# A four-part graph network: the maximum chain two groups ahead, f16 counts, two of twelve scatters behind attention

## The reference

```
h = relu(layernorm(x)); x = x + L0(h)      # graph attention
h = relu(layernorm(x)); x = x + L1(h)      # 5 rounds of sums over edges, product, batch norm
h = relu(layernorm(x)); x = x + L2(h)      # sum over edges by source, mean
h = relu(layernorm(x)); x = x + L3(h)      # message network and a gated unit
# L0, with two head groups (4 heads of 64, 8 heads of 32):
e  = leaky_relu(alpha_s[src] + alpha_d[dst], 0.2)
m  = segment_max(e, dst);  ex = exp(e - m[dst])
a  = ex / segment_sum(ex, dst)
out = segment_sum(h[src] * a, dst)         # then elu, times Wu, plus bias and residual
```

## Time and profile before

| what | value |
|---|---|
| median of 3 runs | 4940.51 us (4921.88 to 4944.49) |
| profiled execution | 4972.68 us, span 4971.0 us |
| TensorE / weight loads | 3609.4 us / 2384.7 us busy |
| VectorE / ScalarE / GpSimd | 2440.7 / 1053.0 / 2126.2 us busy |
| mean granted clock | 0.819 |
| POOL scatters in attention | 384, 647.5 us |
| POOL gathers in attention | 512, 549.6 us |

### The profile page before, as it was taken

One profiled execution on the slowest core, in us unless ns is written; L12 is line 12 of the kernel. 1 busy time (PEld: TensorE's weight loads), 2 busy tenths in 40 slices (PEclk: granted clock), 3 DMA queues, 4 the chain that ended last, 5 costly groups with the idle time before them and its releaser, 6 DMA issues. The chain is left out here.

```text
span 4971.0 us, 63954 instructions
## 1 busy us (share of the span) xinstructions
PE 3609.4 (73%) x15754; PEld 2384.7 (48%) x15755; DVE 2440.7 (49%) x7725; ACT 1053.0 (21%) x2529; POOL 2126.2 (43%) x1886
## 2 busy tenths in 40 slices
PE   5566878777778754511127999999969788888889
PEld 3344555555555543300003555455545555665655
DVE  7766777777777765300001212222155456666656
ACT  0111222222222211200000202122034322222222
POOL 1366878877777850377661000000000055555520
PEclk9967777777777777655558999999979899999999
DMA  9277566556555665311122242322303233333330
GB/s 388 64 181 176 133 135 135 135 132 138 135 130 135 136 119 115 87 52 46 51 67 89 87 122 85 108 85 90 117 17 119 66 93 89 91 90 88 93 68 20
DMA packets 493099, 535.24 MB, mean 108 GB/s; under 512 B 225646, under 2 KB 396236, under 8 KB 492121
## 3 DMA queue, kind: packets, MB, share of 16 engines
q0 software_dynamic: 142000, 250.83, 21.7%
q1 hardware_dynamic: 338300, 266.64, 18.7%
q10 hardware_dynamic: 12749, 17.18, 1.4%
HBM read 470.80 MB, written 104.62 MB: 116 GB/s over the span
## 5 line engine op out<-in xcount | busy, mean ns | idle before, releaser
L1035 PE MATMUL p_out<-rows,hot 128*128 128x266 f32 x2048 | 820.3, 554 | 32.0 <-DVE rows L1157 24.1
L960 POOL DMA_INDIRECT count_dram<-number,place x384 | 647.5, 1686 | 203.7 <-issue 124.1
L1462 PE MATMUL p_lo<-cbuf,parts 128*128 128x400 f16 x1750 | 587.5, 336 | 92.4 <-issue 92.4
L1035 PEld LDWEIGHTS p_out<-rows,hot 128*128 128x128 f32 x2048 | 518.4, 273 | 227.4 <-DVE rows L1157 102.9
L1463 PE MATMUL p_hi<-cbuf,parts 128*128 128x400 f16 x1750 | 587.1, 336 | 47.7 <-issue 47.7
L952 POOL DMA_INDIRECT rows<-att_dram,idx x512 | 549.6, 1074 | 163.3 <-issue 146.8
L2031 POOL DMA_INDIRECT col_rows<-col_dram,m_idx x440 | 417.2, 948 | 435.2 <-ACT m_idx L2101 267.6
L1934 POOL MEMSET attr_w<- 128x512 f32 x1 | 0.5, 525 | 1271.7 <-POOLq L361 1271.7
L1531 POOL DMA_INDIRECT rec_dram<-records,edge_place x416 | 399.1, 959 | 166.6 <-issue 162.0
L1491 DVE TENSOR_TENSOR node_sum<-p_hi,low_sb 128x400 f32<-128x400 f32 x80 | 45.9, 574 | 806.9 <-ACT low_sb L1482 756.9
L1558 PE MATMUL l_p_turn<-wbot,hT 128*128 128x256 f32 x500 | 157.0, 450 | 270.1 <-issue 262.8
(11 more groups left out here) (383 smaller groups left out, 6445.3 us busy)
## 6 DMA issues: line engine op xcount, KB each, us to landing
cbuf<-by_src SPq DMA_DIRECT2D x40, 2500.0 KB
count_dram<-zeros SPq DMA_DIRECT2D x40, 1000.0 KB
dl_rep<-dl_dram SPq DMA_DIRECT2D x128, 256.0 KB
by_src<-count_dram POOLq DMA_DIRECT2D x25, 800.0 KB
g_rows<-by_src SPq DMA_DIRECT2D x25, 800.0 KB, 4.3
key_rep<-key_dram SPq DMA_DIRECT2D x64, 256.0 KB
rec_dram<-blank ACTq DMA_DIRECT2D x1, 14520.0 KB
m_attrs<-rec_dram SPq DMA_DIRECT2D x110, 128.0 KB
```

The costliest lines, as they stand in the source:

```text
L960: nc.gpsimd.indirect_dma_start(count_dram, bass.IndirectOffsetOnAxis(ap=place[r][:, n, c:c + 1].bitcast(U32), axis=0), number[r][:, 2 * n ...
L1035: m = nc.tensor.matmul(p_out[q][:, side, 0:HALF], hot[k][:, u, :], rows[k][:, u, side * HALF:(side + 1) * HALF], start=(u == 0), stop=(u = ...
L1462: nc.tensor.matmul(p_lo[m][:], parts[:, k, m, 1, :], cbuf[q][:, k, :], start=(k == 0), stop=(k == NT - 1))
```

## The change

Three things at once.

1. **Maximum chain.** Group j's pass runs the chain of j+2. TensorE's order in a pass is now: look-up of j+1, turn and turn back of j+2, first product of the sums, tops of j+2, the other products. `scale` has four buffers. The breaks `pen` have a semaphore of their own and are loaded two groups ahead, behind a wait for the scan of g. ScalarE makes the edge matrix of j+2 ahead of the exponential of j. Two groups' chains stand before the loop.
2. **Counts in f16.** `count_dram`, `zeros`, `number` are f16; `zeros` is 4000 wide, so 20 transfers fill the matrix. `by_src` is a view of `count_dram` and the copy goes. `LATE` is -256: a positive number marks the first of its key.
3. **Two of twelve scatters** of each turn (the second pair of k = 2) are kept in `place_post` and `number_post`. 27 of these 32 pairs go out in unify, 5 in the short block, each waiting for the one before. The order in the loop is now 4, 2, 2, 2.

```diff
+FIRSTS = (0, 4, 6, 8)
+IN_LOOP = 10
+POST = 2 * (GROUPS // 4)
+POST_UNIFY = 27
-LATE = 1024.0
+LATE = -256.0
-ZF = 2000
+ZF = 4000
-        zeros = sb("zeros", [P, ZF], F32, early)
+        zeros = sb("zeros", [P, ZF], F16, early)
-        count_dram = dram("count_dram", [KD + TRASH, 1], F32)
-        by_src = dram("by_src", [NP, NP], F16)
+        count_dram = dram("count_dram", [KD + TRASH, 1], F16)
+        by_src = count_dram[0:KD, :].rearrange("(p n) o -> p (n o)", p=NP)
+        def scatter_late(pool, first, last):
+            for n in range(first, last):
+                pool.wait_ge(placed, (CH - POST + 2 * n) * 16)
+                pool.nop().then_inc(waits_passed, 1)
+                for c in range(2):
+                    nc.gpsimd.indirect_dma_start(
+                        count_dram, bass.IndirectOffsetOnAxis(ap=place_post[:, n, c:c + 1].bitcast(U32), axis=0),
+                        number_post[:, n, c:c + 1], None, compute_op=ALU.add).then_inc(placed, 16)
 ...
 (SP)
+                        def breaks(g, q):
+                            for u in range(U):
+                                sp.dma_start(pen[q][u * HW:(u + 1) * HW, :],
+                                             pen_dram[...].partition_broadcast(HW)).then_inc(pen_in[q], 16)
                         def work(g, k, i):
+                            if within(g, 2):
+                                sp.wait_ge(run_ready, g + 1)
+                                sp.nop().then_inc(waits_passed, 1)
+                                breaks(g + 2, q)
                             if not (isinstance(g, int) and g < 2):
                                 sp.wait_ge(keys_used, g - 1)
-                            (four loads of pen)
 ...
 (ScalarE)
                         def work(j, k, i):
+                            if within(j, 2):
+                                edge_hot(j + 2, (k + 2) % 4)
                             act.wait_ge(arg_ready, j + 1)
                             nc.scalar.activation(slots(k), zz[:], ACT.Exp).then_inc(weight_ready, 1)
                             if within(j, 2):
                                 take_scores(j + 2, *after(k, i, 2))
-                                edge_hot(j + 2, (k + 2) % 4)
 ...
 (POOL: "if k % 2 == 0" becomes "if k == 0" for the two pairs of a step)
-                        pool.wait_ge(placed, CH * 16)
+                        pool.wait_ge(placed, (CH - POST) * 16)
 ...
 (TensorE)
                             if within(j, 1):
-                                turn(j + 1)
-                                turn_back(j + 1)
-                                node_tops(j + 1, (k + 1) % 4)
+                                look_up(j + 1, tiles[k])
+                            if within(j, 2):
+                                turn(j + 2)
+                                turn_back(j + 2)
                             if not (isinstance(j, int) and j < 2):
                                 pe.wait_ge(added, j - 1)
-                            for u in range(U - 1):
+                            add_up(j, k, 0)
+                            if within(j, 2):
+                                node_tops(j + 2, (k + 2) % 4)
+                            for u in range(1, U):
                                 add_up(j, k, u)
-                            if within(j, 1):
-                                look_up(j + 1, tiles[k])
-                            add_up(j, k, U - 1)
 ...
 (VectorE, the pass of group j, new order)
+                            if one:
+                                node_hot(j + 1, 1 - q, i1 * 2 + k1 // 2)      # now waits for dl_rep and keys
 ...
                             TS(zz[:], zz[:], 0.0, None, ALU.min).then_inc(arg_ready, 1)
+                            if one:
+                                alike(j + 1, k1, i1, 0)
+                                alike(j + 1, k1, i1, 1)
+                            if two:
+                                run_up(j + 2, q, i2 * 2 + k2 // 2)
+                            dve.wait_ge(weight_ready, j + 1)
+                            weigh(j, k, 0)
+                            n = scale_sums(j - 1, (k + 3) % 4, tile_before) if before else o.skip(1)
+                            if two:
+                                run_ends(j + 2)
+                            weigh(j, k, 1)
 ...
+                                add_sums(j - 1, 1 - q, tile_before)
+                            n = o.did(no_edge(j + 2)) if two else o.skip(1)
+                            weigh(j, k, 2)
+                            n = o.did(node_max()) if two else o.skip(1)
+                            if four:
+                                alike(j + 1, k1, i1, 2)
+                            n = o.did(group_max()) if two else o.skip(1)
+                            weigh(j, k, 3)
+                            n = o.did(with_own(tile_ahead)) if two else o.skip(1)
+                            o.did(edge_places(k, i))
+                            n = o.did(bent()) if two else o.skip(1)
+                            if four:
+                                alike(j + 1, k1, i1, 3)
+                            n = o.did(top_of(tile_ahead)) if two else o.skip(1)
+                            first = o.did(if_first(j + 1, k1, i1))
+                            falls(j + 2, q, tile_ahead)
+                            at_place(k1, i1)       # k1 == 2: second pair to number_post, place_post (two more small instructions)
+                            new_top(j + 2, tile_ahead)
 ...
 (unify, POOL)
-                        for t in range(NT):
-                            pool.dma_start(by_src[t * P:(t + 1) * P, :], counts[t * P:(t + 1) * P, :]).then_inc(narrowed, 16)
-                        pool.wait_ge(narrowed, 16 * NT)
+                        scatter_late(pool, 0, POST_UNIFY)
 (short block, POOL)
+                    scatter_late(pool, POST_UNIFY, POST // 2)
+                    pool.wait_ge(placed, CH * 16)
```

160 lines of the change are left out of this document (76 added, 84 removed).

## The result

The changed kernel took 5104.3 us (median of 4 runs, 5082.7 to 5114.4), the one before 4942.0 on the same chip: ratio 1.034, 95% interval 1.030 to 1.037. It is 3.4% slower; the prediction was 4850, faster. The profiled execution spans 5111.5 us against 4971.0.

What follows compares the result with a forecast made beforehand. The prediction took POOL, taken 96% of the time in attention, as the bound. Its terms, -84 - 3 + 4 + 1 - 5 = -87 us, brought the median from 4940.5 to 4853, stated as 4850, range 4805 to 4895.

Steps and rivals of the forecast that it cites:

- POOL sets the pace; the chain has some 10 us of slack.: Attention loop before the change: POOL, taken 96% of the time, bounds it; VectorE's places are ready some 10 us early.
- The chain, -84 us: Attention, 118 groups: maximum chain two ahead and two scatters out bring a group from 11.86 to 11.15 us, -84 us.
- from there to places and sums 6.7 us, near the full-clock end: New attention loop: from the scan to places and sums takes 6.1 to 8.0 us, taken as 6.7.
- VectorE alone is 10.0: Attention loop: VectorE's own work comes to 10.0 us a group, below POOL's.
- POOL's instructions unchanged: Attention loop: f16 scatters taken as long as f32 ones; denser VectorE work adds about 0.01 us to each POOL instruction.
- Keys on SP: 0: SP's new loading step in attention: lanes and keys there 9.4 us into the group, wanted at 11.3, so 0 us.
- Ahead of the loop, +4: Start of attention and its tail: a second chain ahead of the first places, one less at the tail, +4 us.
- Late scatters: Scatters moved behind attention: covered in unify, ending some 25 us early; five pairs in the short block cost +1 us.
- Zeros, -5: First block: f16 halves the bytes of zeros, so SP ends sooner and VectorE is last, -5 us.
- TensorE starving beside late scatters: Rival 3, unify and next block: TensorE gets one product in 2.8 us beside late scatters, +66 us, 5007; chance 0.05.
- rival 1: Attention: the tighter loop eats the gain, 11.6 to 11.86 us a group, median 4906 to 4940; chance 0.15.
- rival 4: Late scatters: f16 ones land in 3.5 us for 2.2, a late pair takes 7.0, median 4865; chance 0.07.

Runs made afterwards that it cites:

- e9: The f16 counts alone on the kernel before, with all count scatters of attention left out (counts incomplete): 4841.7 us, ratio 0.982.
- e1: The kernel before with only the f16 parts of the change, chain one ahead, twelve scatters in the loop: 4953.5 us, ratio 1.003.
- e2: The kernel before with f16 counts and two late scatters of twelve, chain left one group ahead: 4928.8 us, ratio 0.997.
- e4: The changed kernel with POOL's four gathers of a step ahead of its scatters: 5037.0 us, ratio 1.020.
- e5: The changed kernel with the tops products ahead of the first products, and rhs formed ahead of the scaling of sums: 5009.3 us, ratio 1.011.
- e11: The changed kernel with the edits of e4 and e5 together: 4962.8 us, ratio 1.008.
- e13: e2 with one swap on VectorE, rhs for the tops products formed ahead of the scaling of the sums: 4861.4 us, ratio 0.988.
- e6: The changed kernel with six extra unread products on TensorE ahead of the look-up in each pass: 5123.7 us, ratio 1.035.
- e16: e2 with four extra unread products on TensorE between turn back and tops: 4951.3 us, ratio 1.008.
- e10: The changed kernel with all count scatters of attention and the late ones left out (counts incomplete): 4916.1 us, ratio 0.999.
- e17: The kernel before, f32 counts, with only e13's swap on VectorE, rhs ahead of the scaling of sums: 4941.9 us, ratio 0.998.
- e18: e1 with only e13's swap on VectorE, rhs ahead of the scaling of sums: 4953.1 us, ratio 0.999.
- e12: e2 with TensorE's look-up split: scores looked up behind turn back, running maxima alone behind the chain: 5086.1 us, ratio 1.029.

## Why the prediction was wrong

The forecast was 4850 us, and the time went the other way, to 5104.3. Several steps failed.

**"POOL sets the pace; the chain has some 10 us of slack."** This failed first. POOL was taken 96% of the time, true, but that did not make it the only bound. The prediction measured the slack of the places and not that of the cycle between TensorE and VectorE; with no scatter at all the group is still 11.33 us (e9). So two scatters out of the loop were worth 0.08 us a group (e1 to e2), not the 1.2 that 45.8 + 1.8 to 42.7 us a turn makes.

**The chain, -84 us.** From e2 to the changed kernel it is +1.44 us a group, and 1662.1 - 1496.6 = +165 us of attention. The term that failed is "from there to places and sums 6.7 us, near the full-clock end". The 6.7 went by VectorE's instructions up to the places. The sums that POOL waits for come from TensorE, whose tops and twelve products stand behind the scan in the new order: 9.6 and 10.3 us, and POOL's steps with a wait start 12.7 us apart. "The gaps in TensorE's work that lower its clock shrink" was wrong too: single gaps of up to 4.8 us came, where all but one of e2's are 1.5 us or less, and the clock fell from 0.74 to 0.65. "VectorE alone is 10.0" took no account of the two engines waiting for one another. e4 and e5 give the two parts, the gathers asked for late (0.73) and the tops behind the first products (0.91); they overlap (e11).

**Clock.** From e2 to the changed kernel TensorE's idle time rose by 0.25 us a group and its busy time, for the same instructions, by 1.19 (the products alone from 6.4 to 7.1). So most of the 1.44 is work done at the lower level. The prediction took its chain at the full one. The gains of e4 (10.33 to 9.62), e5 (to 9.19) and e13 (9.14 to 8.79) are in busy time too. Raising the clock by extra work was tried twice (e6, e16), and in both that work took back what the clock gave. No run changed the clock and nothing else, so whether the order costs time by lowering the clock, or the clock follows a loop that is longer for another reason, stays open.

**POOL's instructions unchanged.** A scatter took 1849 ns for 1688, a gather 1132 for 1074. It is neither f16 (e1: 1714) nor the late scatters (e2: 1641); e5, with the same late scatters and chain, has 1708 and 1058. No run tells more. By the Trainium skill, page "SBUF — State Buffer", section "Who interferes with whom", VectorE and GpSimd share a pair of ports, and where both need them the one that issues second waits. VectorE is busy 68% here, for 73% before, so by that rule alone one would look for shorter instructions of POOL. They are longer, so it does not explain this.

**Keys on SP: 0.** Nearly right, 14.9 us of waiting in all. But in e11, nearer 11.9 us, it is 77 us: the cover was the slow loop.

**Ahead of the loop, +4.** It was +14.3. SP issues twelve breaks before the first lanes and keys, and VectorE's queue stands at the hot columns until 278.88. The prediction walked the chain and not SP's queue.

**Late scatters.** Unify as predicted: the last one is over at 2131.7, 24 us before the last addition ends at 2156.2 (25 predicted). The short block: +14.1 for +1. Behind its first pair, sent just after SP's small write at 2168.53, POOL waited 14.6 us; at the 5.7 us of a quiet pair the five would have ended in time. The scatters are not what makes the write slow: SP's next load, which waits for it, comes 15.4 to 16.6 us behind it in before, e1, e9 and e10, where no scatter is near, and 17.4 us behind it here. That the write holds up the pair is likely by this, and not shown.

**Zeros, -5.** Right, by the start of attention: -5.1.

**Rivals.** None held. The slower side came, but not by TensorE starving beside late scatters; the tighter loop was named in rival 1 and bounded at no loss, 11.86 us a group. Its half clock did come; its sum leaves out the loop through TensorE's products.

**Between attention and unify, +9.4, not in the sum.** This goes with the f16 scatters: the signals of the very last one come later, 15.7 to 19.0 us after it for 6.0 and 6.5 (e17, e18). "Masks, sign test and fill cost as before" did not think of it, and rival 4, which had f16 landing slower, looked at the late pairs in unify, where they did not. Why only the last one is late is not known. The last row of the table of stretches, -15.1, is no effect of the change: both values lie within the 2877 to 2925 us that this part takes in all these kernels.

## What to carry over

An engine that is taken 96% is a bound, but not the bound: before trading another engine's slack for it, walk the serial cycle of each engine once round (here TensorE's, turn to turn) and add its waits; leave the suspected work out and see how far the period falls. Where the cycle goes through TensorE, compare its busy time and its idle time apart: the same instructions took 8.79 to 10.33 us a group here by their order alone, and a wait that is made shorter in one place (e13) can come back in another and still pay. One swap here, with two scatters out of the loop, gave 1.2%, where the changed kernel lost 3.4%. And when a dependency is moved one group nearer to its gather, follow it to the last consumer that frees the buffer, on the engine that really ends it.

## What the runs showed of the hardware

TensorE's granted clock in attention ran from 0.65 to 0.78 by order alone, with the same products in all (e6, e12 and e16 have more): 0.65 in the changed kernel, with single gaps of up to 4.8 us and TensorE busy 80% of the time, 0.78 in e13, with gaps of mostly under 1.5 us and TensorE busy 79%. The same instructions took 10.33 us a group in the one and 8.79 in the other.

The last scatter of attention, an accumulating one of 128 single elements, sent its last landing signal 6.0 and 6.5 us after its end with f32 counts and 15.7 to 19.0 us after it with f16. In the loop POOL's waits for landing were no longer with f16 (8.1 us in e1, 37.4 before, from 400 to 1700 us).

A small write on SP's queue held the load behind it for 15.4 to 16.6 us with no scatter near (before, e1, e9, e10). A scatter pair sent 0.8 us after it made POOL wait 14.6 us, where 2.3 was usual.
